# Two expert stages: the last job of each makes its last two second-layer quarters tile by tile, and its normalisations and stores by halves

## The chip, the cores and the metric
The kernel is one program on one core of a Trainium2 chip. The metric is the device time of one execution in microseconds (us); lower is better. All matmuls are float32 data split into a high part (type fp32r) and a low part (what the rounding left over), and each product is made of three matmuls: high by high, high by low, low by high.

## The reference
Over 8192 tokens of width 256 it applies four residual blocks, each `x = x + layernorm(block(layernorm(x)))`: a windowed attention with a memory network, a gate and a dense feed-forward; a mixture of 8 experts with at most 512 tokens each; a linear attention; a mixture of 8 experts with at most 1024 tokens each. The two expert blocks are what the change is about. In short:

```python
# first mixture, per expert e: 512 slots
h = gelu(dispatch[e] @ wi[e])              # 256 -> 1024
combined = weight * (h @ wo[e])[slot]      # 1024 -> 256
out = residual + combined
# second mixture, per expert e: 1024 slots
h = relu(disp[e] @ w1[e] + b1[e])
out = gate_val * (h @ w2[e] + b2[e])[slot]
# both
x = x + layernorm(out)
```

## The kernel before
**Stages.** The program has one hand-written order of work per engine, and semaphores between them. In order of time: the memory network and the dense feed-forward over 16 groups of 512 tokens (16 feed-forward jobs); the first expert stage, `E` = 8 jobs of 512 tokens (n = 0 to 7); the linear attention stage over 16 groups; the second expert stage, 16 jobs of 512 tokens (n = 8 to 23), two for each expert. Tokens reach an expert through DRAM tables of rows (`d_p1`, `d_p2`) that GpSimd has scattered; the result rows are scattered back, after the first stage into `d_x1`, from which the attention stage loads `xA`, after the second into the output.

**A job.** Tokens are transposed to `eh`/`el` (high and low part, two buffers each, by n % 2). The first layer is made in four quarters j of 256 hidden columns, each in two halves k: `expert_in(n, j, k)` is 6 matmuls of 512 columns into a unit of a ring of three PSUM tensors. ScalarE's `hidden` reads it twice, to `fh` (rounded) and `fF` (full), buffers by quarter modulo 2, and VectorE's `low` (L1743) subtracts them into `fl`. The second layer's quarter `w2(job, j)` (L575) waits for the two lows (`low` >= 2n+2) and adds into the PSUM tensor `acc`, for 4 token tiles i of 128 tokens and 256 columns each, 6 matmuls a tile, 24 a quarter; it raises `w2` by one. `acc` tile i is complete only in quarter 3. In `hidden` (L1116) ScalarE waits, before it writes quarter n, for the second-layer quarter n - 2, which reads the same `fh`.

**After the second layer** comes, one job late in VectorE's order: `expert_out` (L1938), which waits for the whole of `w2`, adds `acc` to the residual rows (first stage: four instructions over 128x256; second: one of 128x1024 with the bias `b2e`) into `eq`, and raises `o`; `expert_stats` (L1954), four statistics and four aggregates, raises `evar`; GpSimd's `expert_root` (L2504) makes the factors from the variances, two instructions of 128x4 in the first stage and four behind `evar` in the second, and raises `ers`; `expert_norm` (L1957), four instructions; `expert_sum` (L1962), one of 128x1024 that adds `pay`, and in the first stage another four statistics and aggregates that are stored with the rows; it raises `eres`. Then GpSimd's `expert_put` (L2517) issues four indirect stores (`DMA_INDIRECT`, L2444), one for each 128 rows. In the middle of a stage all this runs beside the next job's matmuls; behind the last job of a stage there is no next job.

**What follows.** SyncE's `load_x1(0)` (L2685) waits until all stores of the first expert stage have landed (`put`), then for each of the 16 groups come GpSimd's `root_l`, ScalarE's `xl_norm` and TensorE's transposes. At the end SyncE waits for `put` too.

**Orders that are touched.** TensorE's loops at L911 and L970, VectorE's at L2282 and L2373 (which ran to `E + 1` and `3 * E + 1`, one round further than there are jobs, for the late work of the last), GpSimd's at L2575 and L2593. In VectorE's first loop `expert_base(n)` writes the residual rows into `eq` before the lows of quarter 3.

Of the kernel before, what the change touches and what calls it, by code (L numbers as in the profile page):

```python
# [70 lines left out]
def f32(ap):  # L71
    return ap.bitcast(F)
# [22 lines left out]
def build(nc, io):  # L95
    ctx = ExitStack()
    with ctx:
# [3 lines left out]
        def dram(name, shape, dt=F):  # L101
# [16 lines left out]

            "etk", "eT", "eh", "etl", "evar", "ers", "eq", "eres", "esu",

# [186 lines left out]
        def weights_free(eng, k, low):  # L307
            if k < 2:
                eng.wait_ge(S["gram"], G - 1 + k)
            elif k < 4:  # L310
                if k == 3 and low:
                    eng.wait_ge(S["w1"], 8 * G)
                else:
                    eng.wait_ge(S["gate"], 2 * G)
            elif k < USE_QKV:
                done = G + (k - 4) // 2
                eng.wait_ge(S["w2"] if k % 2 else S["w1"], (4 if k % 2 else 8) * done)
            elif k == USE_QKV:
                eng.wait_ge(S["lg"], G)
                eng.wait_ge(S["st_df"], 16 * G)  # L320
            else:
                e, second = (k - 19) // 2, (k - 19) % 2
                if e == 1:
                    eng.wait_ge(S["ao"], 2 * G)
                    if second and low:
                        eng.wait_ge(S["lg"], 2 * G)
                else:
                    done = G + E if e == 0 else G + E + 2 * (e - 1)
                    eng.wait_ge(S["w2"] if second else S["w1"], (4 if second else 8) * done)

        def sat_at(g):
# [40 lines left out]
        def tensor_program(pe):  # L372
# [202 lines left out]
            def w2(job, j):  # L575
# [6 lines left out]
                pe.wait_ge(S["low"], 2 * n + 2)  # L582
                gh, gl = fh[n % 2], fl[n % 2]
                for i in range(4):
                    for k in range(2):
# [3 lines left out]
                                  c == 0 and i % 2 == 0, c == 7)  # L589
                t.then_inc(S["w2"], 1)  # L590


# [318 lines left out]
            for n in range(-1, E):  # L911
# [58 lines left out]
            for n in range(E - 1, 3 * E):  # L970
# [8 lines left out]
                if n >= E:  # L979
                    expert_in(n, 2, 0)  # L980
                    expert_in(n, 2, 1)
                    w2(G + n, 1)
                    expert_in(n, 3, 0)
                    expert_in(n, 3, 1)
                    w2(G + n, 2)
                    w2(G + n, 3)

        def scalar_program(act):
# [127 lines left out]
            def hidden(job, j, k, func, bias):  # L1116
                n = 4 * job + j
                u = ring.of("W1", job, j)
                if n >= 2 and k == 0:
                    act.wait_ge(S["w2"], n - 1)  # L1120
                b = 0.0 if bias is None else bias[:, 2 * j + k:2 * j + k + 1]
                act.wait_ge(S["w1"], 8 * job + 2 * j + k + 1)
                act.activation(fh[n % 2][:, half(k)], u.ap[:, half(k)], func, bias=b)  # L1123
                t = act.activation(fF[n % 2][:, half(k)], u.ap[:, half(k)], func, bias=b)  # L1124
                t.then_inc(u.free if k else S["act1"], 1)
# [387 lines left out]
        def vector_program(ve):  # L1513
# [222 lines left out]
            def low(job, j, k):  # L1736
# [4 lines left out]
                else:  # L1741
                    ve.wait_ge(S["act1"], n + 1)
                ve.tensor_tensor(fl[n % 2][:, half(k)], fF[n % 2][:, half(k)], f32(fh[n % 2][:, half(k)]),  # L1743
                                 ALU.subtract).then_inc(S["low"], 1)

# [216 lines left out]
            def expert_sum(n):  # L1962
# [6 lines left out]
                else:  # L1969
                    t.then_inc(S["eres"], 1)  # L1970


# [308 lines left out]
            weights_low(3, 1)  # L2281
            for n in range(-1, E + 1):  # L2282
                now, before, k = 0 <= n < E, 0 <= n - 1, 4 + 2 * n if n + 1 < E else USE_QKV
# [22 lines left out]
                if now:  # L2306
# [6 lines left out]
                    low(G + n, 3, 0)  # L2313
                    low(G + n, 3, 1)
            values_folded()
            for s in range(-1, len(PAIRS) + 2):
# [54 lines left out]
                if s + 1 in PAIRS:  # L2371
                    lows(xAl[(2 * s + 3) % 2], xAh[(2 * s + 3) % 2], ring.of("XLT", 2 * s + 3), S["xlh"], 2 * s + 3)
            for n in range(E - 1, 3 * E + 1):  # L2373
                now, before, k = E <= n < 3 * E, E <= n - 1, 21 + n - E
# [20 lines left out]
                if now:  # L2395
# [4 lines left out]
                    low(G + n, 3, 0)  # L2400
                    low(G + n, 3, 1)

        def pool_program(po):
# [100 lines left out]
            def expert_root(n):  # L2504
# [10 lines left out]
                po.tensor_tensor(t[:, 12:16], b[:, 12:16], w, ALU.mult).then_inc(S["ers"], 1)  # L2515

            def expert_put(n):  # L2517
                if n == 0:
# [55 lines left out]
            scatter(0, 15)  # L2574
            for n in range(E):  # L2575
                expert_root(n)
                expert_put(n)
            for s in range(-2, len(PAIRS) + 2):
                if s + 2 in PAIRS:
# [11 lines left out]
                if s + 2 in PAIRS:  # L2591
                    root_l(2 * s + 5)
            for n in range(E, 3 * E):  # L2593
                expert_root(n)
                expert_put(n)

        def sync_program(sp):
# [293 lines left out]
```

## Time and profile before
| | |
|---|---|
| median of 3 runs | 1931.93 us (1930.73 to 1932.71) |
| the profiled execution's own time | 1932.38 us |
| its span, first to last instruction | 1930.6 us |
| mean granted TensorE clock | 0.958 of full speed |
| TensorE matmuls busy | 1790.9 us (93% of the span) |
| VectorE busy | 1495.8 us (77%) |
| ScalarE busy | 1070.5 us (55%) |
| GpSimd busy | 620.8 us (32%) |

In the page's names PE is TensorE (PEld its weight loads), DVE VectorE, ACT ScalarE, POOL GpSimd, SP SyncE. L374 is the line of the matmul helper, so all matmuls but transposes have it, and operands tell them apart: `ps<-wslotA,fh` is the second layer, `ps<-eh,wslotA` the first. In a timeline a row is one instruction or several alike one after another (xN), its second number the time from the start of the first to the end of the last; in square brackets is how long the engine stood before it and who released it. The ends of matmuls are modelled. Of the 40 slices of the page TensorE is below nine tenths in six: the first, the 20th and 21st, the 25th (behind the first expert stage), the 32nd and 33rd behind the attention stage, and the last.

### The profile page before, as it was taken

The numbers are of one execution on the slowest core, as the hardware profiler recorded it, in microseconds if no ns is written. First come the engines' busy times: TensorE is split into PE (matmuls) and PEld (weight loads), VectorE is DVE, ScalarE is ACT, GpSimd is POOL, SyncE is SP. The second block draws the span as 40 slices with busy tenths as digits, with TensorE's granted clock in tenths as the row PEclk, the third lists the DMA queues.
The fourth block names the chain that finished last, engine by engine and source line by source line (L and its number), as shares of the span: only waits on it lengthen the run. The fifth ranks groups of instructions, "written<-read, shape, count | busy, mean of one in ns | idle before, by whom it ended". The sixth has DMA issues, their size and how long they took to land.

```text
span 1930.6 us, 30931 instructions
## 1 busy us (share of the span) xinstructions
PE 1790.9 (93%) x11218; PEld 1585.3 (82%) x11218; DVE 1495.8 (77%) x3895; ACT 1070.5 (55%) x1733; POOL 620.8 (32%) x921
## 2 busy tenths in 40 slices
PE   6999999999999999999569994989999499999995
PEld 4878888888888888888569994878988499999995
DVE  5777579899999999999748883789998466666653
ACT  4566734566656665665456662565563255555552
POOL 3112001224443333344604443134535312233322
PEclk8999999999999999999779997999999599999998
DMA  4445241223222222201143422134322212222210
GB/s 152 156 145 195 77 143 55 89 90 105 93 83 82 93 69 71 80 27 36 51 151 121 132 86 88 56 121 133 99 87 76 87 59 81 92 88 82 70 56 12
DMA packets 132607, 176.90 MB, mean 92 GB/s; under 512 B 11486, under 2 KB 115813, under 8 KB 132328
## 3 DMA queue, kind: packets, MB, share of 16 engines
q1 hardware_dynamic: 121704, 159.87, 26.1%
q0 software_dynamic: 10752, 15.06, 2.3%
q8 instruction: 89, 1.46, 0.3%
q14 instruction: 62, 0.51, 0.1%
HBM read 113.25 MB, written 76.51 MB: 98 GB/s over the span
## 4 chain that ended last, share of the span: by engine, by line
PE 85%; DVE 5%; issue 3%; ACT 2%; POOL 2%; DMA 2%; SPq 0%; POOLq 0%; DVEq 0%; ACTq 0%
PE ps L374 77%; PE ps L398 4%; PE ps L676 2%; PE ps L665 1%; DVE bst L1529 1%; POOL d_p L2444 1%; PE ps L451 1%; DMA stage<-in_w 0%; DMA wl_t<-in_Wl2T 0%; DVE rO L2014 0%; DMA d_x<-df 0%; DVE pay L1853 0%; SPq L2599 0%; DMA d_p<-pay,sut 0%; DVE wslotA L1734 0%
## 5 line engine op out<-in xcount | busy, mean ns | idle before, releaser
L374 PE MATMUL ps<-wslotA,fh 128*128 128x256 f32 x1792 | 328.8, 284 | 0.0
L1743 DVE TENSOR_TENSOR fl<-fF,fh 128x512 fp32r<-128x512 f32 x320 | 216.9, 684 | 103.2 <-ACT fF L1124 102.2
L374 PEld LDWEIGHTS ps<-wslotA,fh 128*128 128x128 f32 x1792 | 283.0, 191 | 5.3 <-DVE fl L1743 0.2
L374 PE MATMUL ps<-wslotA,fl 128*128 128x256 f32 x896 | 253.4, 283 | 0.0
L2439 POOL TENSOR_TENSOR smalls<-smalls,powers 128x4 f32<-128x4 f32 x88 | 28.2, 321 | 601.9 <-DVE smalls L1532 601.8
L2444 POOL DMA_INDIRECT d_p<-pay,sut x128 | 154.0, 1203 | 106.6 <-DVE pay L1901 53.4
L374 PEld LDWEIGHTS ps<-wslotA,fl 128*128 128x128 f32 x896 | 171.5, 191 | 0.0
L374 PE MATMUL ps<-x2h,wslotA 128*128 128x512 f32 x512 | 171.0, 396 | 0.2 <-DVE x2l L1554 0.2
L1123 ACT ACTIVATE fh<-ps,b1e 128x512 fp32r<-128x512 f32 x128 | 88.3, 690 | 149.1 <-PE ps L374 146.8
L374 PE MATMUL ps<-wslotB,fh 128*128 128x256 f32 x768 | 139.8, 283 | 0.0
L374 PE MATMUL ps<-eh,wslotB 128*128 128x512 f32 x384 | 127.4, 398 | 4.8 <-DVE el L1925 4.8
L374 PE MATMUL ps<-eh,wslotA 128*128 128x512 f32 x384 | 127.7, 399 | 1.4 <-DVE el L1554 1.4
L374 PEld LDWEIGHTS ps<-wslotB,fh 128*128 128x128 f32 x768 | 121.8, 192 | 2.5
L1123 ACT ACTIVATE fh<-ps,cols 128x512 fp32r<-128x512 f32 x128 | 88.7, 693 | 56.3 <-PE ps L374 52.7
L374 PEld LDWEIGHTS ps<-x2h,wslotA 128*128 128x128 f32 x512 | 96.3, 188 | 24.7 <-issue 5.6
L374 PE MATMUL ps<-wslotB,fl 128*128 128x256 f32 x384 | 108.7, 283 | 0.0
L2444 POOL DMA_INDIRECT out_x<-eq,sut x64 | 73.3, 1146 | 95.1 <-DVE eq L1966 79.9
L374 PE MATMUL ps<-x2l,wslotA 128*128 128x512 f32 x256 | 100.2, 391 | 0.0
L2440 POOL TENSOR_TENSOR smalls<-smalls,powers 128x4 f32<-128x4 f32 x88 | 96.5, 1097 | 6.9
L1543 DVE SCALAR_TENSOR_TENSOR xl<-xl,smalls,rows 128x256 f32<-128x256 f32 x192 | 80.1, 479 | 15.6 <-POOL smalls L2440 15.6
L374 PEld LDWEIGHTS ps<-eh,wslotB 128*128 128x128 f32 x384 | 73.5, 191 | 20.0 <-DVE el L1925 5.2
L1529 DVE BATCH_NORM_STATS2 bst<-xl 128x6 f32<-128x256 f32 x256 | 89.5, 412 | 0.3
(346 smaller groups left out, 5021.8 us busy)
## 6 DMA issues: line engine op xcount, KB each, us to landing
stage<-in_w SPq DMA_DIRECT2D x16, 1024.0 KB, 5.4
d_p<-blank SPq DMA_DIRECT2D x24, 528.0 KB, 4.9
pay<-d_p SPq DMA_DIRECT2D x24, 528.0 KB, 3.8
d_x<-df SPq DMA_DIRECT2D x16, 516.0 KB, 3.7
xA<-d_x SPq DMA_DIRECT2D x16, 516.0 KB, 3.8
xa<-in_x SPq DMA_DIRECT2D x16, 512.0 KB, 4.8
d_h<-hh SPq DMA_DIRECT2D x16, 512.0 KB, 5.5
d_h<-hl SPq DMA_DIRECT2D x16, 512.0 KB, 2.7
```

What stands on the lines that cost most here:

```text
L374: return pe.matmul(o, a, b, start=start, stop=stop, skip_group_check=True)
L398: t = pe.transpose(ps[:, c * 512 + i * 128:c * 512 + i * 128 + 128], x[:, i * stride + c * 128:i * stride + (c + 1) * 128], ident)
L451: t = pe.transpose(ps[:, i * 256 + c * 128:i * 256 + c * 128 + 128], x[:, c * 512 + i * 128:c * 512 + i * 128 + 128], ident)
L665: t = pe.transpose(ps[:, c * 512 + i * 128:c * 512 + i * 128 + 128], pv[:, i, c * 128:(c + 1) * 128], ident)
L676: t = pe.matmul(ps[:, i * 8:i * 8 + 8], x[:, c * 512 + i * 128:c * 512 + i * 128 + 128], w8[:, c, :], start=c == 0, stop=c == 1)
L1123: act.activation(fh[n % 2][:, half(k)], u.ap[:, half(k)], func, bias=b)
L1529: marks.append(mark(ve.bn_stats(b[:, i, :], x[:, i, :])))
L1543: marks = [mark(ve.scalar_tensor_tensor(x[:, i, :], x[:, i, :], m[:, i:i + 1], gain, ALU.subtract, ALU.mult)) for i in range(4)]
L1743: ve.tensor_tensor(fl[n % 2][:, half(k)], fF[n % 2][:, half(k)], f32(fh[n % 2][:, half(k)]), ALU.subtract).then_inc(S["low"], 1)
L2439: last(po.tensor_tensor(t[:, 8:12], mv_of(t)[:, :, 1], eps, ALU.add))
L2440: po.tensor_tensor(t[:, 12:16], t[:, 8:12], mhalf, ALU.pow).then_inc(signal, 1)
L2444: po.indirect_dma_start(dst, bass.IndirectOffsetOnAxis(idx[:, i:i + 1], 0), src[:, i, :], None, bounds_check=bound, oob_is_err=False).then ...
```

## The change
For the last job of each stage (`ENDS`):

- **TensorE** makes `expert_in` of quarter 3 before `w2` of quarter 1, and then, in place of `w2(.,2)` and `w2(.,3)`, a new `w2_end`: for each tile i first quarter 2 and then quarter 3, so that `acc` tile 0 is complete first. It waits for all lows of the job at its head. It raises the new semaphore `w2t` after tile 1, and `w2` after tiles 2 and 3.
- **ScalarE** and **VectorE** write quarter 3's `fh` and `fl` into the pair `eh`/`el` of the other parity, so `hidden` waits for a low instead of a `w2`.
- **VectorE** has a new `expert_end`, which is in its order right behind the job's last `low`: adds, statistics and aggregates of tiles 0 and 1 behind `w2t`, then of tiles 2 and 3 behind `w2`; then norm, sum (128x512) and, in the first stage, statistics of tiles 0 and 1, then of 2 and 3. An add and its statistics alternate tile by tile.
- **GpSimd** makes the roots by halves, on 128x2, and the stores by halves: two indirect stores behind `eres_h`, two behind `eres`. In its order both roots stand ahead of the stores.

The count of matmuls, activations and lows is the same. The core of the diff:

```diff
+        ENDS = (E - 1, 3 * E - 1)
+
+        def hid(job, j):
+            n = 4 * job + j
+            if j == 3 and job - G in ENDS:
+                return eh[(job - G + 1) % 2], el[(job - G + 1) % 2], fF[n % 2]
+            return fh[n % 2], fl[n % 2], fF[n % 2]
...
+            def w2_end(job):
+                W = Wt[SLOT[job]]
+                pe.wait_ge(S["low"], 8 * job + 8)
+                for i in range(4):
+                    for j in (2, 3):
+                        gh, gl, _ = hid(job, j)
+                        for k in range(2):
+                            c = 2 * j + k
+                            q = slice(k * 512 + i * 128, k * 512 + i * 128 + 128)
+                            t = three(acc[:, i * 256:(i + 1) * 256],
+                                      [(gh[:, q], gl[:, q], W["w2h"][:, c, :], W["w2l"][:, c, :])], False, c == 7)
+                    if i:
+                        t.then_inc(S["w2t"] if i == 1 else S["w2"], 1)
...
-                    w2(G + n, 1)
-                    expert_in(n, 3, 1)
-                    w2(G + n, 2)
-                    w2(G + n, 3)
+                    if n in ENDS:
+                        expert_in(n, 3, 1)
+                        w2(G + n, 1)
+                        w2_end(G + n)
...
+                    if n in ENDS:
+                        expert_in(n, 3, 0)
+                        expert_in(n, 3, 1)
+                        w2(G + n, 1)
+                        w2_end(G + n)
...
-                if n >= 2 and k == 0:
+                dh, _, df_ = hid(job, j)
+                if k == 0 and j == 3 and job - G in ENDS:
+                    act.wait_ge(S["low"], 2 * (n - 1))
+                elif n >= 2 and k == 0:
                     act.wait_ge(S["w2"], n - 1)
...
+            def expert_end(n):
+                p, first = 16 + n if n < E else 32 + n, n < E
+                q, pv, t = xw(eq[n % 2]), pay_v[p % 3], sm(6, n)
...
+                for h in range(2):
...
+                    if h:
+                        ve.wait_ge(S["w2"], 4 * (G + n) + 4)
+                    else:
+                        ve.wait_ge(S["w2t"], 1 if first else 2)
+                    for i in tiles(h):
+                        a = acc[:, i * 256:(i + 1) * 256]
+                        if first:
+                            o = ve.scalar_tensor_tensor(q[:, i, :], a, pv[:, i, 259:260], q[:, i, :], ALU.mult, ALU.add)
+                        else:
+                            o = ve.tensor_tensor(q[:, i, :], a, b2e[e % 2], ALU.add)
...
+                        marks.append(mark(ve.bn_stats(b[:, i, :], q[:, i, :])))
+                    for i in tiles(h):
+                        ve.wait_ge(*marks[i % 2])
+                        o = ve.bn_aggr(mv[:, i, :], b[:, i, :])
+                    o.then_inc(S["evar"] if h else S["evar_h"], 1)
+                for h in range(2):
+                    r = slice(2 * h, 2 * h + 2)
+                    if h:
+                        ve.wait_ge(S["ers"], n + 1)
+                    else:
+                        ve.wait_ge(S["ers_h"], 1 if first else 2)
+                    for i in tiles(h):
+                        o = ve.tensor_scalar(q[:, i, :], q[:, i, :], mv[:, i, 0:1], t[:, 12 + i:13 + i], ALU.subtract, ALU.mult)
...
+                    o = ve.tensor_tensor(q[:, r, :], q[:, r, :], pv[:, r, 0:256], ALU.add)
+                    if first:
...
+                    o.then_inc(S["eres"] if h else S["eres_h"], 1)
...
-            for n in range(-1, E + 1):
+            for n in range(-1, E):
...
+            expert_end(E - 1)
             values_folded()
...
-            for n in range(E - 1, 3 * E + 1):
+            for n in range(E - 1, 3 * E):
...
+            expert_end(3 * E - 1)
...
+                po.wait_ge(S["esu"], n + 1)
+                for h in range(2):
+                    if h:
+                        po.wait_ge(S["eres"], n + 1)
+                    else:
+                        po.wait_ge(S["eres_h"], 1 if first else 2)
+                    for i in tiles(h):
+                        if first:
+                            po.indirect_dma_start(d_x1, bass.IndirectOffsetOnAxis(sut[:, n % 4, i:i + 1], 0),
...
```

## Rows read from the trace of the kernel before

**Rows 1.** The chain of waits of the whole span, by engine (page, part 4).
```profile
PE 85%; DVE 5%; issue 3%; ACT 2%; POOL 2%; DMA 2%; SPq 0%; POOLq 0%; DVEq 0%; ACTq 0%
```

**Rows 2.** Stretches: from:to, length, busy us (count) by engine, granted clock, DMA share, GB/s.
```profile
1171.00:1196.00 25.00, 2.24 (x13) 1.71 (x12) 8.21 (x26) 3.04 (x9) 8.35 (x14) 0.60 0.33 106
...
1911.00:1930.00 19.00, 0.00 (x0) 0.00 (x0) 5.51 (x14) 0.00 (x0) 5.61 (x8) 0.56 0.01 2
```

**Rows 3.** Timeline of TensorE: start us, duration, engine, line, operation.
```profile
1165.34 0.40 PE L374 MATMUL ps<-wslotA,fh 128*128 128x256 f32 x2
...
1171.10 1.89 PE L374 MATMUL ps<-rows,stage 128*128 128x256 f32 x8
...
1910.61 0.28 PE L374 MATMUL ps<-wslotB,fl 128*128 128x256 f32 x1
```

**Rows 4.** Timeline of VectorE after the first expert stage.
```profile
1171.30 1.66 DVE L1944 SCALAR_TENSOR_TENSOR eq<-ps,pay,eq 128x256 f32<-128x256 f32 x4 [3.94 <-PE ps L374]
1172.99 1.41 DVE L1529 BATCH_NORM_STATS2 bst<-eq 128x6 f32<-128x256 f32 x4
1174.31 0.36 DVE L1532 BATCH_NORM_AGGREGATE smalls<-bst 128x2 f32<-128x6 f32 x4
1176.11 1.38 DVE L1537 TENSOR_SCALAR eq<-eq,smalls 128x256 f32<-128x256 f32 x4 [1.44 <-POOL smalls L2440]
...
1180.11 0.36 DVE L1532 BATCH_NORM_AGGREGATE eq<-bst 128x2 f32<-128x6 f32 x4
```

**Rows 5.** Timeline of GpSimd after the first expert stage.
```profile
1175.04 1.04 POOL L2440 TENSOR_TENSOR smalls<-smalls,powers 128x4 f32<-128x4 f32 x1
1181.33 1.04 POOL L2444 DMA_INDIRECT d_x<-eq,sut  x1 [5.25 <-DVE eq L1532]
...
1185.24 0.97 POOL L2444 DMA_INDIRECT d_x<-eq,sut  x1 [0.30 <-issue]
```

**Rows 6.** Timeline of VectorE at the end.
```profile
1911.03 1.22 DVE L1951 TENSOR_TENSOR eq<-ps,rows 128x1024 f32<-128x1024 f32 x1 [3.85 <-PE ps L374]
...
1913.61 0.36 DVE L1532 BATCH_NORM_AGGREGATE smalls<-bst 128x2 f32<-128x6 f32 x4
...
1917.44 1.23 DVE L1966 TENSOR_TENSOR eq<-eq,pay 128x1024 f32<-128x1024 f32 x1
```

**Rows 7.** Timeline of GpSimd at the end.
```profile
1915.79 0.20 POOL L2515 TENSOR_TENSOR smalls<-smalls,pay 128x4 f32<-128x4 f32 x1
1919.55 1.04 POOL L2444 DMA_INDIRECT out_x<-eq,sut  x1 [3.56 <-DVE eq L1966]
...
1923.46 0.97 POOL L2444 DMA_INDIRECT out_x<-eq,sut  x1 [0.30 <-issue]
```

**Rows 8.** Timeline of ScalarE: the last activation of each of the two jobs.
```profile
1166.04 0.59 ACT L1124 ACTIVATE fF<-ps 128x512 f32<-128x512 f32 x1
...
1905.77 0.68 ACT L1124 ACTIVATE fF<-ps,b1e 128x512 f32<-128x512 f32 x1
```

**Rows 9.** VectorE's groups by form, whole span: shapes, count, busy us, mean ns, idle before.
```profile
L1743 DVE TENSOR_TENSOR fl<-fF,fh 128x512 fp32r<-128x512 f32 x320 | 216.9, 684 | 103.2 <-ACT fF L1124 102.2
...
L1529 DVE BATCH_NORM_STATS2 bst<-eq 128x6 f32<-128x256 f32 x128 | 45.0, 414 | 1.1
...
L1537 DVE TENSOR_SCALAR eq<-eq,smalls 128x256 f32<-128x256 f32 x96 | 33.1, 406 | 6.8 <-POOL smalls L2440 3.8 <-POOL smalls L2515 3.0
...
L1944 DVE SCALAR_TENSOR_TENSOR eq<-ps,pay,eq 128x256 f32<-128x256 f32 x32 | 13.3, 478 | 15.5 <-PE ps L374 15.5
```

**Rows 10.** Timeline of GpSimd and VectorE in an ordinary job of the first stage.
```profile
1137.22 5.32 POOL L2444 DMA_INDIRECT d_x<-eq,sut  x1 [5.73 <-DVE sut L1919]
...
1141.55 1.41 DVE L1934 TENSOR_SCALAR eq<-pay 128x256 f32<-128x256 f32 x4
```

**Rows 11.** Stretches after each restart of TensorE, columns as in rows 2.
```profile
1196.00:1203.00 7.00, 5.59 (x17) 4.41 (x17) 1.38 (x2) 3.15 (x6) 1.55 (x4) 0.50 0.52 136
...
1532.00:1540.00 8.00, 6.59 (x19) 5.13 (x19) 2.08 (x3) 2.46 (x4) 0.00 (x0) 0.50 0.19 67
```

More of the change, by code:

```diff
@@ L582, in w2 @@
                 pe.wait_ge(S["low"], 2 * n + 2)
-                gh, gl = fh[n % 2], fl[n % 2]
+                gh, gl, _ = hid(job, j)
                 for i in range(4):
@@ L1742, in low @@
                     ve.wait_ge(S["act1"], n + 1)
-                ve.tensor_tensor(fl[n % 2][:, half(k)], fF[n % 2][:, half(k)], f32(fh[n % 2][:, half(k)]),
-                                 ALU.subtract).then_inc(S["low"], 1)
+                dh, dl, df_ = hid(job, j)
+                ve.tensor_tensor(dl[:, half(k)], df_[:, half(k)], f32(dh[:, half(k)]), ALU.subtract).then_inc(S["low"], 1)
             def halo(g):
@@ L1970, in expert_sum @@
                     t.then_inc(S["eres"], 1)
+            def expert_end(n):
+                p, first = 16 + n if n < E else 32 + n, n < E
+                q, pv, t = xw(eq[n % 2]), pay_v[p % 3], sm(6, n)
+                mv, e = mv_of(t), max(0, (n - E) // 2)
+                if not first:
+                    ve.wait_ge(put[n % 2], puts(n))
+                    ve.wait_ge(ld_b2[e % 2], 16 * (e // 2 + 1))
+                for h in range(2):
+                    b = bst[:, turns[0] % 2]
+                    turns[0] += 1
+                    marks = []
+                    if h:
[8 more added lines that the diff above has]
+                            o = ve.tensor_tensor(q[:, i, :], a, b2e[e % 2], ALU.add)
+                        if i == 3:
+                            o.then_inc(S["o"], 1)
+                            ve.wait_ge(S["o"], G + n + 1)
+                        else:
+                            last(o)
+                        marks.append(mark(ve.bn_stats(b[:, i, :], q[:, i, :])))
[7 more added lines that the diff above has]
+                        ve.wait_ge(S["ers"], n + 1)
+                    else:
+                        ve.wait_ge(S["ers_h"], 1 if first else 2)
+                    for i in tiles(h):
+                        o = ve.tensor_scalar(q[:, i, :], q[:, i, :], mv[:, i, 0:1], t[:, 12 + i:13 + i], ALU.subtract, ALU.mult)
+                    if h:
+                        o.then_inc(S["eq"], 1)
+                        ve.wait_ge(S["eq"], n + 1)
+                    else:
+                        last(o)
+                    o = ve.tensor_tensor(q[:, r, :], q[:, r, :], pv[:, r, 0:256], ALU.add)
+                    if first:
+                        last(o)
+                        b = bst[:, turns[0] % 2]
+                        turns[0] += 1
+                        marks = [mark(ve.bn_stats(b[:, i, :], q[:, i, :])) for i in tiles(h)]
+                        for i in tiles(h):
+                            ve.wait_ge(*marks[i % 2])
+                            o = ve.bn_aggr(rows258(eq[n % 2])[:, i, 256:258], b[:, i, :])
+                    o.then_inc(S["eres"] if h else S["eres_h"], 1)
@@ L2574, in pool_program @@
             scatter(0, 15)
-            for n in range(E):
+            for n in range(E - 1):
                 expert_root(n)
                 expert_put(n)
+            expert_end(E - 1)
             for s in range(-2, len(PAIRS) + 2):
@@ L2592, in pool_program @@
                     root_l(2 * s + 5)
-            for n in range(E, 3 * E):
+            for n in range(E, 3 * E - 1):
                 expert_root(n)
                 expert_put(n)
+            expert_end(3 * E - 1)
         def sync_program(sp):
```

54 lines of the change are left out of this document (46 added, 8 removed).

## Prediction

> **What bounds the kernel now.** I read first the chain of waits: TensorE carries 85% of it [rows 1], so most of the span is matmul time, which this change neither adds to nor takes from. Then I looked for the stretches where TensorE has nothing to do, because only there can an earlier store be worth something. By stretches there are two behind the jobs that the diff touches [rows 2]: from 1171 to 1196 us TensorE is busy for 2.24 of 25 us, and from 1911 us to the end for 0 of 19. In both a serial tail runs: the last second-layer matmul, then VectorE (add, statistics), GpSimd (root), VectorE (normalise, add), GpSimd (four row scatters); after the first, SyncE's loads of `xA`, which wait for all scatters, then the attention stage; after the second, the end. What the change is worth is how much earlier the fourth scatter of each tail starts.
>
> The landmarks of before, first tail: TensorE begins quarter 2 at 1165.34, leaves the experts at 1171.10 [rows 3]; VectorE starts at 1171.30, has the variances at 1174.67, starts the norm at 1176.11 and ends at 1180.47 [rows 4]; GpSimd's root ends at 1176.08, its scatters start at 1181.33 and, the fourth, 1185.24 [rows 5]. Second tail: last matmul 1910.61 [rows 3]; VectorE starts at 1911.03, variances 1913.97, sum 1918.67 [rows 6]; root ends at 1915.99, scatters start from 1919.55 to 1923.46 [rows 7], and the span ends 7.1 us after that.
>
> **Part 1, TensorE's order.** `expert_in(n,3,1)` (first stage) or both halves of quarter 3 (second stage) go ahead of `w2(.,1)`, and quarters 2 and 3 become one pass by token tiles. 48 matmuls stay 48: in rows 3 they take 1171.10 - 1165.34 = 5.76 us, 1.44 us a tile. Cost taken: zero, and tile 1 is complete 2.88 us ahead of tile 3. What could cost is the wait for the low part of quarter 3 at the head of `w2_end`, behind which the rest of TensorE's program is queued. Before, the second ScalarE pass of (3,1) ended at 1166.63, 1.29 us after its matmuls (1165.34) in the first stage, and at 1906.45, 1.46 us after 1904.99 (1910.75 less 5.76) in the second [rows 8]. VectorE's subtraction adds 0.684 [rows 9] and hand-offs of some 0.03. So low(3,1) is there 2.0 and 2.2 us after its matmuls, and now `w2(.,1)` with 24 matmuls (2.88 us) lies between. Margins: 0.9 and 0.7 us, so zero. Nothing else holds it: quarter 3's operands go to the other, idle `eh`/`el` pair, so ScalarE no longer waits for `w2(.,1)`; `low` of quarter 1, which it waits for now, is long past.
>
> **Part 2, statistics by halves.** Single durations [rows 9]: add 0.478, statistics 0.414, norm 0.406, 512-wide subtraction 0.684. Four statistics after one another take 1.41, so 0.33 each but for the last; four norms 1.38 [rows 4], so 0.73 for two. An instruction waiting for its predecessor starts 0.03 after its end (1176.08 to 1176.11 across engines, rows 4, 5). Half 0: released 2.88 us before half 1, it is done before half 1 starts. Half 1: two adds and two statistics, 0.478+0.03+0.33+0.478+0.03+0.414 = 1.76, two aggregates 0.18 (four take 0.36, rows 4): 1.94 us. First tail: 1171.30+1.94 = 1173.24 (was 1174.67). In the second the add reads a bias row instead; its 1024-wide form takes 1.22 [rows 6], 0.31 a tile, so 0.478 is the upper bound and I take it: 1911.03+1.94 = 1912.97 (was 1913.97).
>
> **Part 3, the roots.** GpSimd does half 0's while VectorE works on half 1. Half 1's I leave at the full width's time, since narrower operands are bounded by 0 and that: 1176.08-1174.67 = 1.41 and 1915.99-1913.97 = 2.02 [rows 4 to 7]. They end at 1174.65 and 1914.99. VectorE meanwhile starts half 0's norm, whose root is ready; that is the overlap.
>
> **Part 4, norm, sum, store by halves.** A half: 0.73+0.03, sum 512 wide 0.684: 1.44 us; in the first stage also two statistics and aggregates, 0.03+0.74+0.18: 2.40. First tail: half 0 from 1173.27 to 1175.67, half 1 to 1178.10 (was 1180.47). Second: half 0 from 1913.00 to 1914.44, half 1 from 1915.02, after its root, to 1916.46 (was 1918.67).
> A scatter starts 0.86 (1180.47 to 1181.33) and 0.88 us after its release, and the fourth 3.91 after the first [rows 4 to 7]. So the first starts at 1176.53 and 1915.32, the fourth at 1180.44 and 1919.23. The third is not held up: half 1 plus 0.86 gives 1178.96 and 1917.32, earlier than the third's turn of 2.6 us after the first. Gains: 1185.24-1180.44 = 4.80 and 1923.46-1919.23 = 4.23 us.
>
> **The new collision.** For the first time these scatters are issued while VectorE works. In an ordinary first-stage job a scatter issued at 1137.22 takes 5.32 us, against 0.97 to 1.04 in the tail; it ends at 1142.54, a scatter's own length after VectorE's two-input subtractions made way, at 1141.55, for a one-input instruction [rows 10]. So a scatter seems not to get through a VectorE instruction that reads two SBUF tensors. Half 1's sum is such a one (1176.46 to 1177.14; 1915.78 to 1916.46). Bound below: no delay. Bound above: the first scatter ends 0.97 after the sum, at 1178.11 instead of 1177.57 and at 1917.43 instead of 1916.36, so 0.5 and 1.1. The row is nearer to a delay, but there the scatter met several such instructions and here one that is half over or not begun: I take the middle, 0.25 and 0.5. Gains 4.55 and 3.7, together 8.3 us.
> The Trainium skill, page "SBUF — State Buffer", section "Who interferes with whom", infers that tensor_tensor takes only the shared read interface while descriptor generation needs the write interface, so such a scatter would not be delayed. By it the sum would be 9.0 us. The trace's 5.32 us scatter disagrees, and the measurement decides.
>
> **What the gain passes through.** After the first tail everything waits in series: loads, GpSimd root, ScalarE norm, transposes. No other wait there ends later, since QKV's low weights were ready before the tail; so all 4.55 us should reach the attention stage, and the expert stage behind it. TensorE restarts there at the lower clock level: 0.50 (1.2 GHz) in 1196 to 1203 and in 1532 to 1540 [rows 11], with 5.6 and 6.6 us of matmuls. The rise to the full level need not keep its distance from the restart. The two stretches differ by some 2 us; at half speed that is 1 us of work, so plus or minus 1 us for the range, zero in the sum.
>
> **Sum.** 1932.38 - 8.3 = 1924.1 for the profiled execution; the median of the runs is 0.45 lower, so the forecast is 1923.6. A measurement here can tell about 0.2%, 3.9 us, from nothing.
>
> **Rivals.**
> (A) VectorE shuts the scatter out until its whole half is done, not only the sum. First tail: first scatter ends at 1178.10+0.97 = 1179.07, the next three start 0.30 later and every 1.28, the fourth at 1181.9: gain 3.3. Second: VectorE's last is the sum, first scatter ends at 1917.43, fourth starts at 1920.3: 3.2. Together 6.5: 1925.4. For it: the 5.32 us row. Against: that scatter ended at 1142.54 while four one-input instructions still ran, from 1141.55 for 1.41 us.
> The skill's same page, section "SBUF: two separate sides", warns of "The DVE blocks DMA trap": a GpSimd-issued DMA starves while VectorE runs a 2-port instruction. It would need the norms to be such instructions, and comes to (A)'s time.
> (B) The first gain is absorbed on the way, for instance by a weight load that is late in the attention stage. Only 3.7 stays: 1928.2. For it: one staged load is on the chain there. Against: SyncE issues it in program order, behind loads that move along.
> (C) The early release is not early, because both halves become ready together: then only the narrower tail after 1171.30 is gained, half 0's 1.94 us come back ahead of half 1's in each tail: 8.3 - 3.9 = 4.4, or 3.6 with the collision at its upper bound. The change then doesn't do what it says: about 1928.
> (D) Slower: TensorE starves at the head of `w2_end`. Granted clocks of 0.60 over 25 us and 0.56 over 19 us [rows 2] are 5.0 and 2.3 us at the full level and the rest at the lower; 2.2 us of the first had matmuls, so the clock falls 2.3 to 2.8 us after they stop. If low(3,1) came so late that TensorE stood for 2.3 us, the 48 matmuls would run at half: +5.8, with the stand 8.1 a stage, 16.2 - 8.3 = +7.9: 1939.8. It decides once low(3,1) is over 0.7 + 4.2 = 4.9 us later than worked out. The ScalarE and VectorE queues hold nothing of that length there.
>
> **How the numbers follow.** Forecast 0.66; A 0.18; B 0.08; C 0.05; D 0.03. Most gain, without the collision: 4.80+4.23+1.0 = 10.0, so 1921.9; least in the forecast and A: 6.5-1.0 = 5.5, so 1926.4. Runs of one kernel spread over 2 us, so 0.7 more at each end: 1921.2 to 1927.1, which leaves out B, C, D. Faster by over 3.9 us: forecast, A and half of B and C, 0.90; within: 0.08; slower: 0.02, D with part of it counted as no change.
>
> **What would show it.** Right: quarter passes by tile with no gap before `w2_end`; in each tail half 0's aggregates about 1 us before the last matmul; fourth scatter 9.1 and 8.2 us, with the collision 9.4 and 8.7, after VectorE takes up half 1, in place of 13.9 (1171.30 to 1185.24) and 12.4 (1911.03 to 1923.46); SyncE's load of `xA` 4.5 us earlier. A first scatter over 1.1 us long shows the collision and its size. Wrong: TensorE idle before `w2_end`; a scatter that starts with half 1's release; a distance from the first tail to the second that has grown.

## The result and the profile after

The changed kernel takes 1923.53 us (median of 6 runs, 1922.07 to 1925.93) against 1931.33 us of the kernel before, measured in turn with it: ratio 0.9961, 95% interval 0.9950 to 0.9972, so 0.4% faster, 5.4 to 9.7 us. Forecast were 1923.6 us and 8.3 us. Its profiled execution has a span of 1921.6 us against 1930.6, 9.0 us less.

First tail. VectorE's timeline of the changed kernel, for [rows 4]:

```profile
1163.08 1.39 DVE L1783 TENSOR_TENSOR el<-fF,eh 128x512 fp32r<-128x512 f32 x2
1168.42 0.48 DVE L2029 SCALAR_TENSOR_TENSOR eq<-ps,pay,eq 128x256 f32<-128x256 f32 x1 [3.94 <-PE ps L385]
...
1170.12 0.30 DVE L2040 BATCH_NORM_AGGREGATE smalls<-bst 128x2 f32<-128x6 f32 x2
1171.30 0.48 DVE L2029 SCALAR_TENSOR_TENSOR eq<-ps,pay,eq 128x256 f32<-128x256 f32 x1 [0.87 <-PE ps L385]
...
1173.00 0.30 DVE L2040 BATCH_NORM_AGGREGATE smalls<-bst 128x2 f32<-128x6 f32 x2
1173.22 0.70 DVE L2049 TENSOR_SCALAR eq<-eq,smalls 128x256 f32<-128x256 f32 x2
...
1175.35 0.30 DVE L2063 BATCH_NORM_AGGREGATE eq<-bst 128x2 f32<-128x6 f32 x2
...
1176.31 0.69 DVE L2055 TENSOR_TENSOR eq<-eq,pay 128x512 f32<-128x512 f32 x1
...
1177.71 0.30 DVE L2063 BATCH_NORM_AGGREGATE eq<-bst 128x2 f32<-128x6 f32 x2
```

Half 0's adds and statistics run from 1168.42 to 1170.42, while TensorE still works on tiles 2 and 3; half 1 is taken up at 1171.30, where the whole `expert_out` was before. GpSimd's timeline, for [rows 5]:

```profile
1173.38 0.27 POOL L2627 TENSOR_TENSOR smalls<-smalls,powers 128x2 f32<-128x2 f32 x1 [1.88 <-DVE smalls L2040]
1173.73 0.74 POOL L2628 TENSOR_TENSOR smalls<-smalls,powers 128x2 f32<-128x2 f32 x1
1176.51 1.43 POOL L2643 DMA_INDIRECT d_x<-eq,sut  x1 [2.03 <-DVE eq L2063]
1178.24 0.97 POOL L2643 DMA_INDIRECT d_x<-eq,sut  x1 [0.30 <-DVE eq L2063]
...
1180.78 0.97 POOL L2643 DMA_INDIRECT d_x<-eq,sut  x1 [0.30 <-issue]
```

The first scatter starts 0.86 us after half 0's aggregates end (1175.65), the second half's pair follows without a pause, and the fourth starts at 1180.78 where it was 1185.24. The first takes 1.43 us and not 1.04: it met the sum of half 1, 1176.31 to 1177.00.

The low parts of quarter 3 end at 1164.47. In TensorE's timeline, for [rows 3], the tile-wise pass (from 1165.33) follows `w2(.,1)` without a gap; this is its tile 0, with `fh` of quarter 2 and `eh` of quarter 3 in turn:

```profile
1165.33 0.40 PE L385 MATMUL ps<-wslotA,fh 128*128 128x256 f32 x2
...
1166.05 0.40 PE L385 MATMUL ps<-wslotA,eh 128*128 128x256 f32 x2
...
1171.09 1.89 PE L385 MATMUL ps<-rows,stage 128*128 128x256 f32 x8
```

It leaves the experts at 1171.09, as before (1171.10).

The end: VectorE's timeline, for [rows 6],

```profile
1903.05 0.42 DVE L2031 TENSOR_TENSOR eq<-ps,rows 128x256 f32<-128x256 f32 x1 [3.86 <-PE ps L385]
...
1905.83 0.42 DVE L2031 TENSOR_TENSOR eq<-ps,rows 128x256 f32<-128x256 f32 x1 [0.89 <-PE ps L385]
...
1907.63 0.70 DVE L2049 TENSOR_SCALAR eq<-eq,smalls 128x256 f32<-128x256 f32 x2
1908.37 0.69 DVE L2055 TENSOR_TENSOR eq<-eq,pay 128x512 f32<-128x512 f32 x1
1909.92 0.73 DVE L2049 TENSOR_SCALAR eq<-eq,smalls 128x256 f32<-128x256 f32 x2 [0.86 <-POOL smalls L2633]
1910.69 0.69 DVE L2055 TENSOR_TENSOR eq<-eq,pay 128x512 f32<-128x512 f32 x1
```

and GpSimd's, for [rows 7]:

```profile
1905.63 0.73 POOL L2632 TENSOR_TENSOR smalls<-smalls,powers 128x2 f32<-128x2 f32 x1
...
1908.46 1.15 POOL L2632 TENSOR_TENSOR smalls<-smalls,powers 128x2 f32<-128x2 f32 x1
1909.69 0.20 POOL L2633 TENSOR_TENSOR smalls<-smalls,pay 128x2 f32<-128x2 f32 x1
1910.50 1.07 POOL L2647 DMA_INDIRECT out_x<-eq,sut  x1 [0.61 <-issue]
...
1914.43 0.97 POOL L2647 DMA_INDIRECT out_x<-eq,sut  x1 [0.30 <-issue]
```

From the release of half 1 to the fourth scatter it is 8.60 us where it was 12.43. Here half 1's norm does wait for its root (0.86 us), and the first scatter starts 0.61 us behind GpSimd's last root instruction. It isn't held up by a sum: it starts at 1910.50, before the sum (1910.69), and takes 1.07. The low parts of quarter 3 end 0.68 us before this stage's tile-wise pass begins (1899.19 and 1899.87), so TensorE doesn't stand here either.

**Where the 9.0 us of the two profiles are.** The first tail gives 13.94 - 9.48 = 4.46. From the fourth scatter to TensorE's restart nothing changes (10.51, now 10.53). From there to the restart behind the attention stage 0.72 are lost (335.75, now 336.47), and from that one to the release of the last half 1.48 are won (379.53, now 378.05). The second tail gives 3.83, and behind it 0.03 are lost. All that the change has in the two middle stretches is TensorE's and ScalarE's new order in the very last job, which order_only below shows to be free. What differs in them is the clock. The chain in order of time of the kernel before,

```profile
1199.10 4.89 PE ps L374 x12
...
1534.88 11.49 PE ps L374 x48
```

and of the changed one:

```profile
1194.66 5.49 PE ps L385 x12
...
1531.16 10.15 PE ps L385 x48
```

The same 12 matmuls after the first restart take 0.60 us more, the same 48 after the second 1.34 less, because the granted clock rises at another distance from the restart ([rows 11] showed the lower level on both). By stretches (columns as in rows 2; the clock is the number behind GpSimd's busy time), first the kernel before, restarted at 1195.75 and 1531.50,

```profile
1202.50:1203.00 0.50, 0.50 (x2) 0.40 (x2) 0.00 (x0) 0.00 (x0) 0.00 (x0) 0.50 1.06 369
1203.50:1204.00 0.50, 0.50 (x5) 0.37 (x4) 0.00 (x0) 0.00 (x0) 0.00 (x0) 1.00 0.05 17
...
1540.50:1541.00 0.50, 0.50 (x2) 0.33 (x2) 0.00 (x0) 0.50 (x2) 0.00 (x0) 0.50 0.00 0
1541.50:1542.00 0.50, 0.50 (x4) 0.40 (x3) 0.29 (x1) 0.18 (x1) 0.00 (x0) 1.00 0.00 0
```

then the changed one, restarted at 1191.31 and 1527.78:

```profile
1199.50:1200.00 0.50, 0.50 (x3) 0.28 (x2) 0.00 (x0) 0.00 (x0) 0.19 (x1) 0.50 0.00 0
1200.50:1201.00 0.50, 0.50 (x6) 0.50 (x5) 0.38 (x1) 0.09 (x1) 0.50 (x1) 1.00 0.00 0
...
1534.00:1534.50 0.50, 0.50 (x3) 0.40 (x2) 0.00 (x0) 0.31 (x1) 0.00 (x0) 0.50 0.00 0
1535.00:1535.50 0.50, 0.50 (x4) 0.42 (x3) 0.01 (x1) 0.46 (x1) 0.00 (x0) 1.00 0.00 0
```

The rise from 0.50 (1.2 GHz) to 1.00 (2.4 GHz) comes some 7.4 us after the first restart before and 8.7 after the change, and some 9.6 and 6.7 us after the second. By the tails alone the change is worth 8.3 us; 0.76 of the 9.0 fall to the two middle stretches, where the clock differs. (Behind the attention stage only the 32nd slice of the page before is below nine tenths, not the 33rd; besides the slices named above, the 27th is at eight tenths.)

### The profile page after: what moved, and what is told of

The parts are those of the page before. It is cut to its first block, busy times and chain, and to the rows that moved or that the text cites. A ratio compares the mean times of both kernels' runs of the same rounds, so it can differ in the third digit from the quotient of the medians.

```text
span 1921.6 us, 30942 instructions
## 1 busy us (share of the span) xinstructions
PE 1790.6 (93%) x11218; PEld 1585.2 (82%) x11218; DVE 1497.3 (78%) x3900; ACT 1070.8 (56%) x1733; POOL 624.1 (32%) x927
## 4 chain that ended last, share of the span: by engine, by line
PE 86%; DVE 5%; issue 3%; ACT 2%; POOL 2%; DMA 2%; SPq 0%; POOLq 0%; DVEq 0%; ACTq 0%
PE ps L385 77%; PE ps L409 4%; PE ps L701 2%; PE ps L690 1%; POOL d_p L2540 1%; DVE bst L1568 1%; PE ps L462 1%; DMA stage<-in_w 0%; DMA wl_t<-in_Wl2T 0%; DVE rO L2108 0%; DMA d_x<-df 0%; DVE pay L1892 0%; SPq L2735 0%; DMA d_p<-pay,sut 0%; DVE wslotA L1773 0%
```

## The experiments

Times are medians, each with the ratio to the kernel before as measured in turn with it. The runs were not all made on one chip, and the kernel before took 1930.6 to 1934.2 us beside them, so ratios compare and times don't. The last two rows are single runs, beside a kernel before of 1934.18. All tails are read from traces, from VectorE's release of half 1 (or of the whole `expert_out`) to the start of the fourth scatter.

| kernel | time, us | ratio, 95% interval | first tail | restart to restart | restart to last release | second tail |
|---|---|---|---|---|---|---|
| before | | | 13.94 | 335.75 | 379.53 | 12.43 |
| changed | 1923.5 | 0.9961 (0.9950 to 0.9972) | 9.48 | 336.47 | 378.05 | 8.60 |
| s1_only | 1927.0 | 0.9973 (0.9964 to 0.9983) | 9.48 | 335.75 | 377.94 | 12.43 |
| s2_only | 1927.5 | 0.9976 (0.9966 to 0.9987) | 13.92 | 336.50 | 377.87 | 8.61 |
| late_release | 1927.3 | 0.9978 (0.9969 to 0.9987) | 11.38 | 336.46 | 379.37 | 10.45 |
| whole_store | 1927.7 | 0.9977 (0.9968 to 0.9986) | 11.48 | 336.68 | 377.95 | 10.34 |
| order_only | 1930.0 | 0.9999 (0.9990 to 1.0008) | 13.92 | 334.96 | 377.98 | 12.41 |
| by_tile | 1922.4 | 0.9953 (0.9939 to 0.9966) | 8.49 | 336.30 | 378.05 | 8.60 |
| delay2 | 1926.6, one run | | 11.31 | 336.84 | 378.17 | 8.60 |
| delay4 | 1927.5, one run | | 13.48 | 336.05 | 378.73 | 8.61 |

**s1_only and s2_only: the change in one stage.** `ENDS = (E - 1,)` or `ENDS = (3 * E - 1,)`, the other stage's loops and tails as before.

> The change for the first expert stage alone (the last job of the second stage as before). By my theory the tails are independent: the first restart of TensorE comes 4.4 us earlier than before, as in the changed kernel, and the end as much earlier, give or take 1 us for where the clock rises after the two restarts: 4.4 (3.4 to 5.4) us faster than before. Rival B (the first gain is absorbed on the way) expects the restart 4.4 earlier but the end under 2 us earlier. Rival C (only the narrower tail counts) expects 2.5.

> The change for the last job of the program alone. No restart of TensorE moves, so the clock has no part in it: last matmul where it was before (within 1 us), fourth scatter 8.6 us after VectorE takes up half 1 in place of 12.4, so 3.8 us faster than before. The rival that the end's gain is partly the clock's expects clearly less, under 3.

s1_only: 0.27% is 5.2 us; s2_only: 0.24% is 4.6 us, with intervals of some 2 us to either side. The traces are sharper. Each tail is what it is in the changed kernel, and the other what it was before, so the two gains are independent and add: 4.46 and 3.82 us. The ratios are too coarse to show it: 0.27% and 0.24% are 0.51% together, against 0.39% (0.28% to 0.50%). In s1_only TensorE's restart came at 1191.85, 3.9 us before that of the kernel before (1195.75) and not the 4.4 expected, as the scatters' landing and the loads took 0.6 longer in that execution; the end kept the gain: the span of 1925.1 is 5.5 less, 3.9 of them the restart's and 1.6 won behind the second restart, where the clock differs (377.94 against 379.53). Nothing absorbs the gain: rival B falls, which allowed under 2 us. For s2_only I had said that the clock has no part, since no restart moves. That was wrong: the stretch from restart to last release was 377.87 us and not 379.53, and 1.50 of the 1.66 lie in the 48 matmuls (9.99 and 11.49), far ahead of the one edited job. The place of the clock's rise can so differ without any edit ahead of it.

**order_only: the reorder with the old tails.**

```diff
-            expert_end(E - 1)
...
-            expert_end(3 * E - 1)
...
```

> TensorE's and ScalarE's new order alone; the adds, statistics, roots and stores as before the change. My theory: no gap of TensorE ahead of the tile-wise pass, tails of 13.9 and 12.4 us as before, so no difference from before beyond 1 us (the clock at the two restarts). Rival D expects TensorE to stand there and to be slower than before.

Ratio 0.9999, both tails as before. TensorE's order alone neither costs nor gives anything; rival D falls.

**late_release: the halves without the tile order's head start.**

```diff
-                        ve.wait_ge(S["w2t"], 1 if first else 2)
+                        ve.wait_ge(S["w2"], 4 * (G + n) + 4)
```

> The changed kernel, but VectorE's half 0 waits for the whole second layer instead of tiles 0 and 1, so the tile order of TensorE brings nothing and only the halves remain. My theory: half 0's 1.94 us (1.84 in the second tail) come back in each tail, fourth scatter 11.4 and 10.5 us after the last matmul's release in place of 9.5 and 8.6: 3.8 us slower than the changed kernel, some 4 faster than before. Rival (the halves alone do it, TensorE's order is decoration): within 1 us of the changed kernel.

11.38 and 10.45 us (here from half 0's release, which is the last matmul's): 1.90 and 1.85 us of each tail come back, as worked out, 3.75 together; the two ratios, measured at different times, differ by 0.17%, 3.3 us. So the tile order is worth 3.75 us of the 8.3, although it gives nothing alone: it is the precondition, and the halves turn it into time. This kernel is what rival C described (4.4 us expected, 4.5 measured in the tails); the changed kernel isn't it.

**whole_store: four scatters behind the second half.**

```diff
-                    if h:
-                        po.wait_ge(S["eres"], n + 1)
-                    else:
-                        po.wait_ge(S["eres_h"], 1 if first else 2)
+                    po.wait_ge(S["eres"], n + 1)
```

> The changed kernel, but GpSimd starts its four scatters only behind the second half's sum. My theory: first scatter 0.86 us after VectorE's end, at 7.6 and 6.4 us after the release of half 1 in place of 5.2 and 4.7, the fourth 3.9 later, and no scatter longer than 1.1 us, since none meets VectorE: 3.6 us slower than the changed kernel. Rival (the scatters are held off by VectorE anyway, so that early ones bring little): within 1.5 us of the changed kernel.

11.48 and 10.34 us: 2.00 and 1.74 more, together 3.7, as expected; the ratio is 0.16% above the changed kernel's, 3.1 us. The first scatter starts 7.57 and 6.45 us after half 1's release and takes 1.05 and 1.04. So early stores are worth 3.7 us even with their collision.

**dve_two, dve_one, two_dense, one_dense: what VectorE work holds a scatter up?** Five VectorE instructions of 128x1024 on idle tiles behind its last sum, beside the last three scatters: additions of two tensors or multiplications of one; in the first pair each waits for the one before (0.03 us of gap), in the second they write different tiles and run without a gap. The edit of two_dense:

```diff
+            for dst in (etk, ef, fh[1], fl[1], eh[1]):
+                ve.tensor_tensor(dst, fF[0], fF[1], ALU.add)
```

> The changed kernel with five extra 1024-wide VectorE additions of two SBUF tensors behind its last sum, beside the last three scatters; what they compute is not used. They take 6.3 us, so VectorE ends 1.3 us or so after the scatters would. If such instructions hold a scatter off, at least one of the three takes over 1.4 us and the fourth starts 1 to 4 us later than 8.6 us after half 1's release. If a scatter needs only what these instructions leave free (the rival), all three take 0.97 to 1.1 us and the time is the changed kernel's.

> The same with five 1024-wide VectorE multiplications of one SBUF tensor by a constant in place of the additions. If only a second input tensor is what collides: scatters of 0.97 to 1.1 us, fourth at 8.6 us. If VectorE runs these at twice the rate (0.6 us each instead of 1.2) and then keeps GpSimd out, as the Trainium skill, page SBUF - State Buffer, says of such instructions: scatters longer than 1.3 us here.

> As dve_two, but the five additions write different tiles and wait for nothing, so there is no gap between them. In dve_two a scatter met a two-input instruction and ended 0.8 to 0.9 us after that instruction's end: 0.03 us of gap let it through. If that is the mechanism, the second scatter now ends 0.8 to 0.95 us after the last of the five, some 6 us after its start, and the fourth starts 4 to 5 us later than in dve_two. Rival (each scatter loses at most some 0.5 us, whatever runs beside it): the same times as dve_two within 0.5 us.

> As dve_one, but without gaps between the five one-input multiplications (0.74 us each with their gaps there, against 1.25 for the additions). If these too keep GpSimd out while they run, the second scatter ends 0.8 to 0.95 us after the last of them, about 4 us after its start. If only a second input tensor is what collides: all scatters 0.97 to 1.2 us, as in dve_one.

dve_two: only the second scatter was held up, to 1.49 us; the others took 0.97 and 0.98, and the fourth started 9.11 us after the release, 0.5 later and not the 1 to 4 that I expected. dve_one: 1.04, 1.15 and 1.15, between what the two ideas had expected (up to 1.1, or over 1.3). GpSimd's timeline of two_dense,

```profile
1911.46 1.49 POOL L2649 DMA_INDIRECT out_x<-eq,sut  x1 [0.30 <-issue]
1913.26 1.96 POOL L2649 DMA_INDIRECT out_x<-eq,sut  x1 [0.30 <-issue]
1915.53 1.97 POOL L2649 DMA_INDIRECT out_x<-eq,sut  x1 [0.30 <-issue]
```

and VectorE's:

```profile
1910.89 1.22 DVE L2499 TENSOR_TENSOR etk<-fF,fF 128x1024 f32<-128x1024 f32 x1
1912.03 1.22 DVE L2499 TENSOR_TENSOR ef<-fF,fF 128x1024 f32<-128x1024 f32 x1
1913.16 1.22 DVE L2499 TENSOR_TENSOR fh<-fF,fF 128x1024 fp32r<-128x1024 f32 x1
1914.30 1.22 DVE L2499 TENSOR_TENSOR fl<-fF,fF 128x1024 fp32r<-128x1024 f32 x1
1915.43 1.22 DVE L2499 TENSOR_TENSOR eh<-fF,fF 128x1024 fp32r<-128x1024 f32 x1
```

The scatters (in all four kernels the second to fourth of the tail) end at 1912.95, 1915.22 and 1917.50: 0.84, 0.84 and 0.85 us after the end of the addition that was running when they started (1912.11, 1914.38, 1916.65). None waited for the whole run of additions. My expectation of a scatter of 6 us is refuted: each of these waited only for the one addition that it met, although the next stood ready. In dve_two too the scatters end 0.84 to 0.87 us after the addition that ran at their start; the third and fourth lost nothing because only 0.1 us of it was left, not because of the gap. The rival (at most 0.5 us each) falls too: with 1.22 us instructions the price is up to 1.0 each. The four times, 1923.3, 1923.1, 1925.4 and 1924.8 us, are single runs and decide nothing here.

In one_dense VectorE's multiplications take 0.67 to 0.84 us, against 1.22 for an addition, and the scatters 1.03, 1.05 and 1.05. One of them and the multiplication that it met:

```profile
1914.49 1.05 POOL L2649 DMA_INDIRECT out_x<-eq,sut  x1 [0.30 <-issue]
...
1913.87 0.84 DVE L2499 TENSOR_SCALAR fh<-fF 128x1024 fp32r<-128x1024 f32 x1
```

It ends 0.83 us after the multiplication (1915.54 and 1914.71), and so do the other two (1914.18 and 1913.35; 1916.90 and 1916.07); in dve_one it is 0.84 to 0.85. These scatters were held like the others, and the price was at most 0.18 us only because they met a multiplication with 0.20 to 0.30 us left. A second input tensor is therefore not what it takes. Not everything on VectorE holds a scatter: in the kernel before one that started at 931.12, with 0.42 us of a statistics instruction left, took 0.97 us, and in by_tile the first scatter started with 0.33 us of a 256-wide norm left and took 1.05.

The 5.32 us scatter of [rows 10] did wait for a run. These are the first and the last of the five two-input subtractions beside it, which follow one another without a gap:

```profile
1136.93 1.22 DVE L1925 TENSOR_TENSOR el<-ef,eh 128x1024 fp32r<-128x1024 f32 x1
...
1140.94 0.68 DVE L1743 TENSOR_TENSOR fl<-fF,fh 128x512 fp32r<-128x512 f32 x1
```

It ended 0.92 us after the last (1142.54 and 1141.62). Six scatters of the kernel before, each the first of its job, took 5.30 to 5.32 us in this way. Why they waited through the run and those of two_dense didn't stays open; none of these experiments put the first scatter of a group against such a run.

The Trainium skill, page "SBUF — State Buffer", section "Who interferes with whom", infers that tensor_tensor leaves descriptor generation alone; the 1.96 us scatters disagree. These are indirect ones, which also read row numbers from the SBUF tile `sut`, and no run here tells the two apart. The box on "The DVE blocks DMA trap" in its section "SBUF: two separate sides" says that 2-port instructions starve it; the scatters of one_dense, ended 0.83 us after a 1024-wide multiplication of 0.77 or 0.84 us, agree with it, if that is such an instruction, which the trace doesn't say.

**delay2 and delay4: is time ahead of a restart passed on one to one?** Two or four idle GpSimd roots behind the first half's release, in the first tail.

```diff
                         po.wait_ge(S["eres_h"], 1 if first else 2)
+                        if first:
+                            for _ in range(2):
+                                last(po.tensor_tensor(b[:, 0:4], epsc, mhalf, ALU.pow))
```

> The changed kernel with two idle GpSimd roots (1.04 us each) behind the first half's release in the first tail: its fourth scatter 1.5 to 2.2 us later than the changed kernel's (9.5 us after half 1's release). What I claim of the clock: the time from TensorE's restart to the end isn't constant, because the clock's rise keeps no fixed distance from the restart: the 12 matmuls of the first restart take anything from 4.6 to 5.5 us and the 48 of the second 9.9 to 11.5, so that the end comes between 0.3 and 4 us later. Rival: a delay ahead of the restart is passed on one to one, and both stretches take what they took in the changed kernel, 5.49 and 10.15, within 0.2.

> The same with four idle roots: fourth scatter 3.7 to 4.5 us later than the changed kernel's. By the clock's part the end comes 2.2 to 6 us later, with the two stretches again somewhere in 4.6 to 5.5 and 9.9 to 11.5; by the rival 3.7 to 4.5 later, with 5.49 and 10.15.

The fourth scatter came 1.83 and 4.00 us later than in the changed kernel, the spans grew by 3.2 and 4.2 (of which +0.4 and -0.4 lie ahead of the tail). The chain in order of time of delay4:

```profile
1198.60 4.39 PE ps L385 x12
...
1534.68 10.85 PE ps L385 x48
```

In delay2 the two stretches took 5.49 and 10.31. The first is the changed kernel's within 0.2, the second too; delay4's 4.39 is 1.1 less and its 10.85 is 0.7 more. So the one-to-one rival falls by delay4's stretches, though not by its end, which at 4.2 us later is what that rival expected too. The 4.39 also lies below the 4.6 to 5.5 that I had given. Over all fourteen kernels the 12 matmuls took 4.39 to 5.49 us and the 48 took 9.94 to 11.49 (11.49 in the kernel before, 11.41 in late_release, 10.85 or less in all others).

How much of this is chance is open. The changed kernel and the four dve kernels are the same up to the very last instructions; their five profiles differ by 0.6 us from restart to restart (335.84 to 336.47), but only by 0.1 from the second restart to the last release (377.96 to 378.06). A single profile of two different kernels is in any case no measure of 1 us; the tails, read from event to event, are.

**by_tile: finer still, in the first tail.** Norm, sum, statistics and store of one tile each, the next tile's norm put between a tile's statistics and its aggregate.

```diff
...
+                    for i in range(4):
+                        ve.wait_ge(*m)
+                        last(ve.tensor_tensor(q[:, i, :], q[:, i, :], pv[:, i, 0:256], ALU.add))
+                        s = mark(ve.bn_stats(bst[:, i % 2, i, :], q[:, i, :]))
...
+                        if i < 3:
+                            m = normed(i + 1)
...
```

> The changed kernel with the first tail's norm, sum, statistics and stores tile by tile instead of by halves (the second tail stays by halves, since its first scatter waits for GpSimd's second root, not for VectorE). By my theory the first scatter's release comes 0.7 us earlier (one tile's norm, sum, statistics and aggregate, about 1.7 us, in place of two tiles' 2.4) and the stores follow one another: fourth scatter 8.4 us after half 1's release in place of 9.5, so 1.1 us faster than the changed kernel, 0.3 if each of the scatters is held off by a sum. Rival: the extra waits on VectorE eat it, fourth scatter at 9.3 to 9.8.

8.49 us, 0.99 less than the changed kernel's 9.48, and its time is the lowest of all, 1922.4 us, ratio 0.9953. GpSimd's timeline:

```profile
1176.13 1.05 POOL L2668 DMA_INDIRECT d_x<-eq,sut  x1 [1.17 <-DVE eq L2062]
1177.48 1.06 POOL L2668 DMA_INDIRECT d_x<-eq,sut  x1 [0.30 <-issue]
...
1180.13 0.97 POOL L2668 DMA_INDIRECT d_x<-eq,sut  x1 [0.30 <-issue]
```

The first scatter starts 4.49 us after half 1's release and not 5.21, the 0.7 that was expected. No scatter is over 1.06 us: the sums are now 256 wide, 0.42 us, and the first scatter began before the one it overlaps (1176.49), which gives the rest. The intervals of the two ratios overlap, so as a time the 1 us isn't shown; the tail shows it.

## Why the prediction was right

**The bound.** Right: of what the change touches only the two tails moved, by what their chains gave; SyncE's first load of `xA` starts at 1183.37 where it was 1187.78. From the first tail's fourth scatter to the second tail's release it is 725.05 us, before 725.79: the distance has not grown, although its first part has, by the clock.

**Part 1.** Right. The margin ahead of `w2_end` was put at 0.9 us in the first stage and is 1165.33 - 1164.47 = 0.86, in the second at 0.7 and is 0.68; order_only shows cost zero. Rival (D) was priced with a slip that changes nothing here: by its own condition, a stand of 2.3 us, it would have set in with low(3,1) 3.0 us late, not 4.9.

**Part 2.** 1.94 us a half were worked out, 2.00 and 1.88 measured: two aggregates after fresh statistics take 0.30 and not 0.18, and in the second tail the add takes 0.42, below the 0.478 taken as its bound.

**Part 3.** Too long in the first tail, for nothing: from variances to factors 1.17 us (1173.30 to 1174.47) and not 1.41, but VectorE comes for them only at 1175.57. Too short in the second: 2.18 and not 2.02 (1907.71 to 1909.89), on the path there. A narrower root is quicker (0.73 against 1.04), but half 1's in the second tail took 1.15, in every kernel with that tail. It started while half 0's sum ran (1908.46, the sum from 1908.37 to 1909.06). In the first tail the same power started during the norm (1173.73), ahead of the sum (1173.96), and took 0.74. So it seems to be held like a scatter, by what runs when it starts; I had left that out of the sum.

**Part 4.** First tail: first scatter 1176.53 worked out, 1176.51 measured. Second: 4.29 us after half 1's release worked out, 4.67 measured. The step that was mis-sized is "a scatter starts 0.88 us after its release", which forgets that GpSimd makes half 1's root first: half 0 was released at 1909.06 and would have allowed 1909.94, but GpSimd's own arithmetic ended only at 1909.89, and a scatter starts 0.61 us after that, at 1910.50.

**The collision.** Right in kind in the first tail: 0 to 0.5 us taken as 0.25, measured 1.43 - 1.04 = 0.39. In the second I took 0.5 and there was none. The scatter of the first tail ended 0.94 us after the sum that it met (1177.94 and 1177.00), near the 0.97 of the upper bound; that of the second started before its sum. The reasoning from the 5.32 us row, that a scatter can't pass a run of two-input instructions, is only half right: six scatters of the kernel before waited through such a run, those of two_dense for one addition each. And a second input isn't the condition, as one_dense shows. Rival (A) would have given tails of 10.6 and 9.3 us; 9.48 and 8.60 were measured.

**The sum.** 4.55 and 3.7 were forecast, 4.46 and 3.83 came: 8.3 twice. In the second tail two errors of 0.4 to 0.5 us cancelled. The measured ratio allows 5.4 to 9.7, so it can't tell these terms apart, and the profiled pair's 9.0 has 0.76 of the clock in it, which the plus or minus 1 us of the forecast had set aside.

## What to carry to other kernels

Where an engine stands idle behind the last job of a stage, read the serial tail event by event and ask of each step for which half of its data it could start sooner; the gain is the head start only if every later step, the stores too, is cut the same way (tile order alone 0, with halves but late stores 4.6, all of it 8.3 us). Price the issue of stores on their own: four GpSimd scatters took 3.9 us from first to last start where their data was there and nothing held them (4.3 in the changed first tail). And don't judge a change of 1 us by one profile's span when the clock must rise again behind an idle stretch.

## What the runs showed of the hardware

- A GpSimd scatter took 0.97 to 1.05 us alone. One that started during a 1024-wide VectorE addition of two SBUF tensors ended 0.84 to 0.87 us after that addition (up to 1.97 us long), and one that started during a 1024-wide multiplication by a constant 0.83 to 0.85 after it; the first of a group, during a 512-wide sum, 0.94 after it.
- This is no rule without exception: in the kernel before 61 of 72 indirect DMAs that started with over 0.17 us left of a VectorE operation on two SBUF tensors ended 0.83 to 0.94 us after it, three were not held, and eight waited longer, six of them through a run of five (5.30 to 5.32 us).
- A GpSimd power of 128x2 took 0.73 us alone, 0.74 when it started during VectorE's norm, and 1.15 when it started during the 512-wide sum.
- A 1024-wide multiplication by a constant took 0.67 to 0.84 us on VectorE, an addition of two tensors 1.22.
- Behind a stop of TensorE the same matmuls took 9.94 to 11.49 us in fourteen profiles: the granted clock's rise to the full level kept no fixed distance from the restart (some 9.6 us in the kernel before, 6.7 in the changed one), and it moved in s2_only, which has no edit ahead of it.
